# A graph transformer layer with routed experts: x1 and y stored four graphs side by side and loaded four at a time, eight more y tiles kept on chip

## The reference

```python
scores = x.mean(axis=1) @ router_w + router_b
top1 = jnp.argmax(scores, axis=-1)
W = expert_w[top1]
support = jnp.einsum('bnh,bhk->bnk', x, W)
out = jnp.einsum('bnm,bmk->bnk', adj, support)      # y in the kernel
# mean and var of out per expert, over its graphs and their nodes
y = (out - m) * inv * bn_gamma[top1][:, None, :] + bn_beta[top1][:, None, :]
x = _layernorm(x + relu(y))
```

## Time and profile before

| what | us |
|---|---|
| median of the three timed runs (2798.2 to 2800.65) | 2800.11 |
| the profiled execution | 2796.44 |
| its span, first to last instruction | 2794.7 |
| TensorE busy | 2679.6 (96%) |
| VectorE busy | 2007.6 (72%) |
| ScalarE busy | 1512.3 (54%) |
| GpSimd busy | 1277.2 (46%) |
| bytes moved | 277.32 MB, 99 GB/s over the span |

### The profile page before, as it was taken

The page is one execution under the profiler, slowest core; times in us unless marked ns, Lnnn a source line. Parts: engine busy times, 40 slices in busy tenths (PEclk is TensorE's granted clock), DMA queues, the critical chain, the costliest instruction groups (busy, mean ns, idle before and its releaser), DMA issues. The chain is left out here.

```text
span 2794.7 us, 77903 instructions
## 1 busy us (share of the span) xinstructions
PE 2679.6 (96%) x22583; PEld 2263.7 (81%) x22584; DVE 2007.6 (72%) x8351; ACT 1512.3 (54%) x5391; POOL 1277.2 (46%) x1174
## 2 busy tenths in 40 slices
PE   8999999999999999999999999999689999997776
PEld 7888888888888888888888888888578888884232
DVE  6788888888888888888878887888633333334887
ACT  5565555556565656565656565656444444442444
POOL 2333333333333333334333433333256666666887
PEclk9999999999999999999999999999899999998999
DMA  4111111111111111111111111111144444445999
GB/s 146 62 53 53 53 61 53 53 53 61 54 52 56 57 57 49 61 53 57 49 64 51 55 53 61 53 53 53 55 131 133 137 133 137 133 137 189 395 406 348
DMA packets 169427, 277.32 MB, mean 99 GB/s; under 512 B 19378, under 2 KB 52146, under 8 KB 168882
## 3 DMA queue, kind: packets, MB, share of 16 engines
q1 hardware_dynamic: 150962, 243.36, 26.3%
q10 hardware_dynamic: 18432, 33.56, 3.1%
HBM read 184.57 MB, written 92.27 MB: 99 GB/s over the span
## 5 line engine op out<-in xcount | busy, mean ns | idle before, releaser
L512 POOL TENSOR_TENSOR probs<-probs,row_scale 128x512 f32<-128x512 f32 x512 | 532.6, 1040 | 1092.6 <-DVE row_scale L408 1092.4
L316 ACT ACTIVATE probs<-neg_s,neg_max 128x128 f32<-128x128 f32 x2048 | 793.3, 392 | 138.8 <-DVE neg_max L384 138.8
L384 DVE CUSTOM_DVE_ANT_0 neg_s<-att_bank,adj_nat 128x128 f32<-128x128 f32 x2048 | 442.6, 285 | 4.3 <-PE att_bank L197 2.4
L316 ACT ACTIVATION_READ_ACCUMULATOR probs<-neg_s,neg_max 128x1 f32 x2048 | 390.7, 191 | 0.0
L393 DVE TENSOR_REDUCE abs_max<-neg_s 128x4 f32<-128x512 f32 x512 | 349.0, 682 | 0.1
L176 PE MATMUL att_bank<-xt_hi,att_w_hi 128*128 128x256 f32 x2048 | 329.5, 283 | 11.0 <-DVE att_w_lo L366 11.0
L176 PE MATMUL att_bank<-xt_hi,att_w_lo 128*128 128x256 f32 x2048 | 330.0, 283 | 0.0
L176 PE MATMUL att_bank<-xt_lo,att_w_hi 128*128 128x256 f32 x2048 | 329.5, 283 | 0.0
L176 PEld LDWEIGHTS att_bank<-xt_hi,att_w_hi 128*128 128x128 f32 x2048 | 298.9, 191 | 30.5 <-issue 10.6
L344 ACT ACTIVATE probs_t<-att_bank 128x512 f32<-128x512 f32 x256 | 153.1, 598 | 299.3 <-PE att_bank L235 299.2
L176 PEld LDWEIGHTS att_bank<-xt_hi,att_w_lo 128*128 128x128 f32 x2048 | 283.1, 192 | 0.0
(11 more groups left out here) (133 smaller groups left out, 5370.2 us busy)
## 6 DMA issues: line engine op xcount, KB each, us to landing
xt_stage<-in_x_t SPq DMA_DIRECT2D x64, 512.0 KB, 3.5
x_nat<-in_x SPq DMA_DIRECT2D x128, 256.0 KB, 2.6
x_scratch<-x SPq DMA_DIRECT2D x128, 256.0 KB, 2.0
g_x<-x_scratch SPq DMA_DIRECT2D x128, 256.0 KB, 2.8
n_x<-x_scratch SPq DMA_DIRECT2D x128, 256.0 KB, 5.9
out_x<-n_x ACTq DMA_DIRECT2D x128, 256.0 KB, 5.5
y_scratch<-g_out SPq DMA_DIRECT2D x96, 256.0 KB, 2.0
n_y<-y_scratch SPq DMA_DIRECT2D x96, 256.0 KB, 5.6
```

Source lines behind the costliest of these rows:

```text
L316: nc.scalar.activation(probs[:, h * P:(h + 1) * P], neg_s[:, h * P:(h + 1) * P], ACT.Exp, bias=neg_max[:, h:h + 1], scale=-1.0, accum_out= ...
L384: nc.vector.tensor_tensor_reduce(neg_s[:, h * P:(h + 1) * P], bank[r][:, c * P:(c + 1) * P], adj_nat[:, s], -2.0, BIG, ALU.add, ALU.min, n ...
L512: nc.gpsimd.tensor_tensor(part, part, by, ALU.mult).then_inc(probs_done, 1)
```

## The change

The two scratch tensors get another layout: `x1_scratch` is `[32, 128, 4, 512]`, so that the four graphs of a quad lie side by side in each partition, and `y_scratch` is `[32, 128, 3, 512]`. Stores in the first two stages still write one tile, now as 128 rows of 2 KB that lie 8 KB (x1) or 6 KB (y) apart. The loads of x1 in the expert stage still read one tile.

In the final stage SP loads a quad at a time: one transfer for four x1 tiles (1 MB, rows of 8 KB) and one for the quad's y tiles that were not kept (three, or two in each fourth quad). The semaphores `tiles_in` and `stored` count for quads, not for places.

Kept are now the graphs with t mod 4 = 3, and besides them those with t mod 16 = 14, eight in all, which lie in `w_stage` (as `more_kept`). 88 tiles are stored and loaded instead of 96. A kept tile is scaled where it lies, and TensorE reads it there; the ring `y` has 12 tiles instead of 16. In the expert stage the instructions of sixteen graphs are written out in the loop body, since which graphs are kept now repeats after sixteen.

```diff
 def is_kept(s):
-    return s % KEPT_EVERY == KEPT_EVERY - 2
+    return s % KEPT_EVERY == KEPT_EVERY - 1 or s % SPAN == SPAN - 2      # SPAN = 16
+
+def kept_tile(kept, more_kept, s, quad, span):
+    if s % SPAN == SPAN - 2:
+        return more_kept[:, bass.ds(span, 1), :].rearrange("p a n -> p (a n)")
+    return kept[:, bass.ds(quad, 1), :].rearrange("p a n -> p (a n)")
...
# attention_phase, sync
-                sp.dma_start(x1_dram[t], x1[:, s]).then_inc(x1_out[s], 16)
+                sp.dma_start(x1_dram[i][:, s], x1[:, s]).then_inc(x1_out[s], 16)
...
# expert_phase
-    ROUNDS = 2
+    ROUNDS = SPAN // UNROLL
...
-                if not is_kept(s):
+                if not is_kept(place):
                     sp.wait_ge(out_done, t + 1)
-                    sp.dma_start(y_dram[t], out[:, s]).then_inc(out_stored[s], 16)
+                    sp.dma_start(y_dram[i][:, s], out[:, s]).then_inc(out_stored[s], 16)
...
# norm_phase
-        y = sb("n_y", [P, RING, D])
+        y = sb("n_y", [P, QUADS, KEPT_EVERY - 1, D])
...
+        def y_tile(s, i):
+            if is_kept(s):
+                return kept_tile(kept, more_kept, s, i * QUADS + s // UNROLL, i)
+            return y[:, s // UNROLL, s % UNROLL]
...
-            def load_y(t, s):
-                sp.dma_start(y[:, s], y_dram[t]).then_inc(tiles_in[s], 16)
-
-            def load_x1(t, s):
-                sp.dma_start(x1[:, s], x1_dram[t]).then_inc(tiles_in[s], 16)
-
-            for s in range(RING):
-                if not is_kept(s):
-                    load_y(s, s)
-                load_x1(s, s)
+            def load_y(quad, u):
+                n = sum(not is_kept(u * UNROLL + k) for k in range(UNROLL))
+                sp.dma_start(y[:, u, 0:n], y_dram[quad][:, 0:n]).then_inc(tiles_in[u], 16)
+
+            def load_x1(quad, u):
+                sp.dma_start(x1[:, u * UNROLL:(u + 1) * UNROLL], x1_dram[quad]).then_inc(tiles_in[u], 16)
+
+            for u in range(QUADS):
+                load_y(u, u)
+                load_x1(u, u)
 
             def body(t, s, i, last):
-                if not last:
-                    if not is_kept(s):
-                        sp.wait_ge(sum_ps, t + 1)
-                        load_y(t + RING, s)
-                    sp.wait_ge(stored[s], i * 16 + 16)
-                    load_x1(t + RING, s)
+                if not last and s % UNROLL == UNROLL - 1:
+                    u = s // UNROLL
+                    sp.wait_ge(sum_ps, t + 1)
+                    load_y((i + 1) * QUADS + u, u)
+                    sp.wait_ge(stored[u], (i + 1) * UNROLL * 16)
+                    load_x1((i + 1) * QUADS + u, u)
...
-                pe.matmul(dst, ident[:, :], y[:, s], start=True, stop=False)
+                pe.matmul(dst, ident[:, :], y_tile(s, i), start=True, stop=False)
...
-                    dve.wait_ge(tiles_in[place], (i + 1) * (16 if is_kept(place) else 32))
+                    dve.wait_ge(tiles_in[place // UNROLL], (i + 1) * 32)
...
-                if is_kept(s):
-                    pool.wait_ge(z_done, t + 1)
-                    src = kept[:, bass.ds(i * QUADS + s // UNROLL, 1), :].rearrange("p a n -> p (a n)")
-                else:
-                    pool.wait_ge(tiles_in[s], i * 32 + 32)
-                    src = y[:, s]
-                nc.gpsimd.tensor_tensor(y[:, s], src,
+                if not is_kept(s):
+                    pool.wait_ge(tiles_in[s // UNROLL], (i + 1) * 32)
+                tile = y_tile(s, i)
+                nc.gpsimd.tensor_tensor(tile, tile,
                                         mul_row[:, bass.ds(e, 1), :].rearrange("p a n -> p (a n)"),
                                         ALU.mult).then_inc(scaled_done, 1)
...
-                act.dma_start(out_dram[t], x1[:, s]).then_inc(stored[s], 16)
+                act.dma_start(out_dram[t], x1[:, s]).then_inc(stored[s // UNROLL], 16)
...
# build
-    x1_dram = nc.dram_tensor("x1_scratch", [B, P, D], F32, kind="Internal").ap()
-    y_dram = nc.dram_tensor("y_scratch", [B, P, D], F32, kind="Internal").ap()
+    x1_dram = nc.dram_tensor("x1_scratch", [B // UNROLL, P, UNROLL, D], F32, kind="Internal").ap()
+    y_dram = nc.dram_tensor("y_scratch", [B // UNROLL, P, KEPT_EVERY - 1, D], F32, kind="Internal").ap()
...
+        more_kept = w_stage[:, :, :, :].rearrange("p a c d -> p (a c) d")
```

More of the change, by code:

```diff
@@ L31 @@
 KEPT_EVERY = UNROLL
+SPAN = 4 * UNROLL
 GROUP = 2
@@ L606, in for_steps, with stores_ahead @@
             rounds(B // (ROUNDS * UNROLL) - 1, True)
+        def stores_ahead(s, place, span):
+            a_span = sum(not is_kept(n * UNROLL + s) for n in range(ROUNDS))
+            return span * a_span + sum(not is_kept(n * UNROLL + s) for n in range(place // UNROLL))
         def exists(step, last, ahead):
@@ L614, in _, with load @@
         def _(sp):
-            def load(t, s):
-                sp.dma_start(x1[:, s], x1_dram[t]).then_inc(x1_in[s], 16)
+            def load(t, s, quad):
+                sp.dma_start(x1[:, s], x1_dram[quad][:, s]).then_inc(x1_in[s], 16)
                 sp.dma_start(adj_t[:, s, 0:P], io["adj_t"][t]).then_inc(adj_in[s], 16)
-            load(0, 0)
+            load(0, 0, 0)
             sp.dma_start(router_w[:, :, :], io["router_w"].rearrange("(c p) e -> p c e", p=P)).then_inc(router_in, 16)
             sp.dma_start(router_b[:, :], io["router_b"].unsqueeze(0)).then_inc(router_in, 16)
-            load(1, 1)
+            load(1, 1, 0)
             for e in range(2, E):
@@ L626, in _, with body @@
             for s in range(2, UNROLL):
-                load(s, s)
-            def body(t, s, i, last, ends):
+                load(s, s, 0)
+            def body(t, s, i, last, ends, place, span):
                 if exists(t, last, UNROLL):
                     sp.wait_ge(y_ps, t + 1)
-                    load(t + UNROLL, s)
-                if not is_kept(s):
+                    load(t + UNROLL, s, i + 1)
+                if not is_kept(place):
                     sp.wait_ge(out_done, t + 1)
-                    sp.dma_start(y_dram[t], out[:, s]).then_inc(out_stored[s], 16)
+                    sp.dma_start(y_dram[i][:, s], out[:, s]).then_inc(out_stored[s], 16)
             for_steps(sp, body)
-            for s in range(UNROLL):
-                if not is_kept(s):
-                    sp.wait_ge(out_stored[s], 16 * (B // UNROLL + 1))
+            for s in range(KEPT_EVERY - 1):
+                sp.wait_ge(out_stored[s], 16 * (stores_ahead(s, 0, B // SPAN) + 1))
         @block.tensor
@@ L726, in body @@
                 act.wait_ge(out_ps, t + 1)
-                if is_kept(s):
-                    dst = kept_tile(i)
+                if is_kept(place):
+                    dst = kept_tile(kept, more_kept, place, i, span)
                 else:
-                    act.wait_ge(out_stored[s], i * 16 + 16)
+                    act.wait_ge(out_stored[s], stores_ahead(s, place, span) * 16 + 16)
                     act.wait_ge(sum_done, t + 1)
@@ L822, in body @@
                 acc = out_sum[:, bass.ds(e, 1), :].rearrange("p a n -> p (a n)")
-                src = kept_tile(i) if is_kept(s) else out[:, s]
+                src = kept_tile(kept, more_kept, place, i, span) if is_kept(place) else out[:, s]
                 nc.gpsimd.tensor_tensor(acc, acc, src, ALU.add).then_inc(sum_done, 1)
@@ L885, in norm_phase @@
         into_done, quad_begun = sem("into_done"), sem("quad_begun")
-        tiles_in = [sem(f"n_tiles_in{i}") for i in range(RING)]
-        stored = [sem(f"stored{i}") for i in range(RING)]
+        tiles_in = [sem(f"n_tiles_in{i}") for i in range(QUADS)]
+        stored = [sem(f"stored{i}") for i in range(QUADS)]
         scaled_done, sum_ps, z_done = sem("scaled_done"), sem("n_sum_ps"), sem("z_done")
@@ L1135, in body @@
                 act.wait_ge(out_done, t + 1)
-                act.dma_start(out_dram[t], x1[:, s]).then_inc(stored[s], 16)
+                act.dma_start(out_dram[t], x1[:, s]).then_inc(stored[s // UNROLL], 16)
             for_steps(act, body)
-            for s in range(RING):
-                act.wait_ge(stored[s], 16 * (B // RING))
+            for u in range(QUADS):
+                act.wait_ge(stored[u], 16 * (B // QUADS))
 def build(nc, io, out_dram, B, D, E):
     C = D // P
-    x1_dram = nc.dram_tensor("x1_scratch", [B, P, D], F32, kind="Internal").ap()
-    y_dram = nc.dram_tensor("y_scratch", [B, P, D], F32, kind="Internal").ap()
+    x1_dram = nc.dram_tensor("x1_scratch", [B // UNROLL, P, UNROLL, D], F32, kind="Internal").ap()
+    y_dram = nc.dram_tensor("y_scratch", [B // UNROLL, P, KEPT_EVERY - 1, D], F32, kind="Internal").ap()
     with ExitStack() as ctx:
```

14 lines of the change are left out of this document (5 added, 9 removed).

## The result

| kernel | median us | lowest to highest | executions |
|---|---|---|---|
| before | 2799.15 | 2797.82 to 2800.65 | 4 |
| changed | 2835.16 | 2831.69 to 2836.28 | 4 |

The ratio on record is 1.0135, 95% interval 1.0123 to 1.0147 (the two medians as they stand give 1.0129): the changed kernel is 36 us slower. The prediction was 2797.9 us with a range of 2789 to 2808. The profiled execution of the changed kernel took 2835.45 us with a span of 2833.2.

A forecast was written before the change was run, and what follows sets the result against it. The prediction took the final stage as bound by the DMA engines (7.12 us a quad), GpSimd just behind at 7.00. With a burst cycle of 7.1 it took 7.05, saving 2.2 us: 2797.9 us, range 2789 to 2808.

The forecast's parts named there:

- rival B: Final stage: SP's wait for the fourth store, then GpSimd's for the megabyte, bind; +6.5 us, 2806.6 us; chance 0.22.
- One wait for a whole quad: Final stage: x1 loads wait for a quad's fourth store, GpSimd for the megabyte; 3.2 us a turn to spare for queueing.
- ring sum: Final stage, one turn of four quads: fixed steps plus unhindered store and load, T + 17.9 us, must stay below 4T.
- drift argument: Final stage: with the period above the bursts' cycle of 7.1 us, load bursts drift earlier, away from the stores, leaving slack.
- calculation by order of issue: Final stage: transfers served in order of issue give a burst cycle of 7.27 us, 6.7 with two y tiles, 7.1 average.
- Longer rows: Final-stage loads in 8 or 6 KB rows take 6% less engine time; DMA need between 6.69 and 6.94 us a quad.
- estimate that the prediction made from the Trainium skill's rule: Final-stage queues: a store waits for an entire x1 share (2.44 us) but not for the y behind it.
- Scalings: GpSimd, final stage: a kept tile costs 1275 ns, another 1271, so scaling in place changes nothing, 0.
- Nothing for the expert stage: Expert stage: eight fewer stores beside a full TensorE are worth 0; the sixteen graphs written out 0, within 1 us.
- balance of DMA engines and GpSimd: Final stage, per quad: DMA engines need 7.10 us, GpSimd 7.00; lighter transfers can free 3.5 us at most.
- Rival C: Final-stage loads: rows are cut to 2 KB anyway, DMA need 6.94 us a quad, 2798 to 2800 us; chance 0.05.
- Rival A: Final stage: GpSimd's issue gap shrinks too, period 6.80 us, -9.4 us, 2790.7 us; chance 0.25.

The follow-up runs named there:

- x1_short_rows: The changed kernel with x1_scratch laid out tile after tile, still one 1 MB transfer a quad but in rows of 2 KB: 2837.95 us.
- kept_only: The kernel before with only the new choice of kept tiles, scaled in place, and sixteen graphs written out; layouts and transfers as before: 2794.23 us.
- x1_by_tile: The changed kernel with x1 loaded tile by tile (256 KB), each once its own store has landed, y still by the quad: 2793.81 us.
- x1_four_at_once: The changed kernel with four 256 KB x1 loads issued together after the quad's four stores, GpSimd waiting for each tile by itself: 2818.49 us.
- y_alone: The changed kernel with GpSimd's scaling waiting for y only, and VectorE waiting for x1 where it adds it: 2808.52 us.
- four_at_once_y_alone: The changed kernel with four 256 KB x1 loads issued together after a quad's four stores, and GpSimd waiting for y only: 2798.41 us.
- x1_by_tile_y_alone: The changed kernel with x1 loaded tile by tile, each on its own store, and GpSimd waiting for y only: 2792.83 us.
- no_y_loads: The changed kernel with no y transfers in the final stage after the first sixteen graphs, stale y tiles being used again: 2810.47 us.

## Why the prediction was wrong

**The mechanism was named, as rival B, and the forecast went the other way.** Place and order are B's: SP's wait for the fourth store, then GpSimd's for the megabyte, once a quad. It was given 0.22 and 6.5 us; it cost 36.

**The step that failed is the queueing in "One wait for a whole quad".** The fixed part of the ring sum held: 17.9 less the 2.09 and 4.4 us for an unhindered store and load is 11.4, and its longest step, from nb to the fourth store, took 5.10 us on average where 5.20 were summed. The chain above then adds 8.23 + 8.72 = 17.0, and (11.4 + 17.0) / 3 = 9.5 us for that turn. The mean period of 8.46 us means 3 x 8.46 - 11.4 = 14.0 us for the pair, and the landings measured over all turns give 13.5, with some 0.3 us more for what starts behind each. That is 7.0 to 7.5 above the 6.5 of an unhindered pair, where 3.2 were to spare. Two terms made it so:

- The prediction's rival B let the last store meet a part of the bursts, 3.9 to 4.5 us with the load's share (with the two more stores that it names, 3.9 + 1.3 is 5.2 and not 4.5, and T 7.7 us). The last store alone lost 4.7 us, landing after 6.8, and in the longest turns it landed with all the loads beside it, after 8 to 9.5. I had the earlier trace rows at hand: 5.5 and 6.1 us for tiles of 256 KB, 6.8 us above unhindered for the pair. With that alone B gives (17.9 + 6.8) / 3 = 8.2 us, close to the 8.46 measured. I took this number as a sign for B, and then priced B by an idealised queue instead.
- A megabyte was summed at 4.4 us though its own row had 5.2. In the ring none landed in less than 5.2, the mean is 6.8, and without y traffic 6.1.

**The drift argument is wrong.** It said that bursts move away from the stores once T is above their cycle. In a closed ring the burst is started by the store, so it can't drift from it: in the rows above x1 goes out 0.14 us after the last store has landed, and the next quad's stores are issued into it. The calculation by order of issue kept the engines at 406 GB/s, and so left out that a ring which waits leaves them empty now and then: their share was 0.06 from 2575 to 2576 us and 0.39 from 2622 to 2623. In the first of these turns the burst also started slowly. Three of the windows after an x1 load issued at 2575.69:

```profile
2576.00:2577.00 1.00, 0.70 (x3) 0.08 (x1) 0.78 (x2) 0.51 (x1) 1.00 (x2) 1.00 0.14 49
2577.00:2578.00 1.00, 0.94 (x3) 0.49 (x3) 1.00 (x3) 0.46 (x2) 1.00 (x1) 1.00 1.16 197
...
2579.00:2580.00 1.00, 1.00 (x4) 0.49 (x3) 0.97 (x6) 0.80 (x1) 1.00 (x2) 1.00 1.07 385
```

**Longer rows** had the wrong sign as read: 365 GB/s per unit of share against 387, not 410. x1_short_rows shows that the fall isn't due to the length of x1's rows, and that the gain of 6% isn't there: 362 per unit of share with long rows, 354 with short ones (2600 to 2780 us). The 410 came from the first microseconds of the kernel, where only loads run.

**The order in which transfers are served.** By the estimate that the prediction made from the Trainium skill's rule (DMA: Bandwidth & Descriptors, Queues, rings and completion order), a store isn't held up by the y queued behind x1, and B doesn't decide. The landings above speak against that estimate. The same section of the Trainium skill also says that the semaphore's increment, which completes a DMA, lands only after the earlier writes of its engine, across its queues. That agrees with stores landing together with the loads beside them, but it can be only the smaller part here: from a last store's last packet to its landing pass at most 1.0 us on average, 0.4 for a store alone, and the other 4.1 us of the delay are its data's. The Trainium skill's rule for most bandwidth, a megabyte or more a DMA (DMA: Bandwidth & Descriptors, Rules for kernel authors), didn't pay here: 2835.16 us by the megabyte, 2793.81 by 256 KB.

**What held.** Scalings of 1.268 to 1.272 us, in place too. Nothing for the expert stage, its end and the start of the final stage. The balance of DMA engines and GpSimd, 7.10 against 7.00: it set the most that could be won at 3.5 us, and kept_only and x1_by_tile won 2.5 and 2.9, the first with an interval that reaches 1. Rival C is out: the long packets are there. Rival A didn't come true, for GpSimd's gap for "issue" is still 23.2 us in kept_only; but the DMA engines are at 404 GB/s there too, so whether lighter DMA traffic would shorten the gap stays open.

**Settled and open.** Shown: release and arrival by quads cause the loss (by tile 2794, by pair 2808, by quad 2835), with 14 to 17 us of it through the arrival in one piece (x1_four_at_once) and 23 to 27 through GpSimd's needless wait (y_alone), shares that overlap. Release by quads alone, with both remedies in, costs nothing against the kernel before (four_at_once_y_alone) and some 5 us against x1_by_tile_y_alone. y's traffic deepens the loss by 22 to 25 us (no_y_loads). Not shown: how much the slow start of a burst adds, and why a load's packets are heavier in a megabyte than in single tiles.

## What to carry to other kernels

Count a ring in units of its release, and sum one turn of it: the last store of a unit, then the whole transfer of the next. For both take the landing times of the loaded engines, in the stage itself; if they fill the turn, small transfers that follow each other tile by tile win over large ones. Let only the engine that reads a buffer wait for it, above all where another one runs ahead in order. The DMA engines already ran at 406 GB/s with 256 KB transfers here, and larger ones gained nothing.

## What was unexpected of the hardware

- A store of 256 KB lets SP load again after 2.09 us when it is alone, and lands after 9.5 and 9.7 us beside 1.75 MB of loads on another queue, of which 768 KB were issued after it in the second case. Much of that time passes before its own packets move: for 2 us, 2613.4 to 2615.4, its queue had none.
- Rows of 8 KB instead of 2 KB for x1's megabyte didn't change the kernel's time (2835.16 against 2837.95 us), though the megabyte landed after 6.8 instead of 7.5 us on average.
- After a pause the engines moved 49 and 197 GB/s in the first two whole microseconds of a megabyte's load, and 385 two later. After another (issue at 2622.70) it was 279 and 301, so the slow start isn't the same each time.
